# Norm factors moved into the phases before, the first token list moved ahead, and the first feed-forward's weights loaded behind the rows

## The reference

```
x = x + 0.5 * ffn(layernorm(x))
x = x + attention(layernorm(x))          # 16 heads of 16, rotary, causal
x = x + 0.5 * ffn(layernorm(x))          # the same weights as in the first

layernorm(x) = (x - mean) / sqrt(var + 1e-5)          # per token
ffn(x):   probs = softmax(x @ gate_w.T)               # 8 experts
          the two best experts of each token, their weights scaled to sum 1
          out = sum over both of weight * (silu(x @ w_gate[e]) * (x @ w_up[e])) @ w_down[e]
```

## Time and profile before

| what | value |
|---|---|
| median of 3 runs | 1222.4 us (1221.09 to 1222.83) |
| the profiled execution, its own time | 1221.54 us |
| its span (first to last instruction) | 1219.8 us |
| mean granted clock of PE | 0.906 of full speed |
| busy in the span: PE, DVE, ACT, POOL | 82%, 69%, 52%, 48% |
| SP's stores of rows (L350) | 64 of 128 KB |
| indirect DMAs: gathers, scatters | 142, 142 (both feed-forwards) |

### The profile page before, as it was taken

The page is one execution under the profiler, slowest core; times in us unless marked ns, Lnnn a source line. Parts: engine busy times, 40 slices in busy tenths (PEclk is TensorE's granted clock), DMA queues, the critical chain, the costliest instruction groups (busy, mean ns, idle before and its releaser), DMA issues. The chain is left out here.

```text
span 1219.8 us, 24054 instructions
## 1 busy us (share of the span) xinstructions
PE 1005.3 (82%) x6998; PEld 644.4 (53%) x6998; DVE 846.4 (69%) x2632; ACT 629.8 (52%) x1318; POOL 586.2 (48%) x756
## 2 busy tenths in 40 slices
PE   1639998973888389999999999999988569998850
PEld 1428987873767223333333333333348349988750
DVE  5595443434999498989998989898529784444437
ACT  1604544443777206666666666666775505544430
POOL 0937777764999402222222222222239227777740
PEclk9857999996999659999999999999989859999975
DMA  6803333324565521111111111110023413333349
GB/s 216 272 0 105 104 104 102 103 100 149 155 180 165 155 66 44 60 59 57 58 60 58 56 59 56 56 55 2 2 59 85 139 35 104 104 103 104 105 149 329
DMA packets 84524, 121.19 MB, mean 99 GB/s; under 512 B 10920, under 2 KB 63920, under 8 KB 81200
## 3 DMA queue, kind: packets, MB, share of 16 engines
q1 hardware_dynamic: 63424, 75.08, 19.7%
q0 software_dynamic: 13632, 37.24, 9.5%
q10 hardware_dynamic: 7344, 7.34, 1.8%
HBM read 75.51 MB, written 43.78 MB: 98 GB/s over the span
## 5 line engine op out<-in xcount | busy, mean ns | idle before, releaser
L1353 ACT ACTIVATE a_probs<-a_ps_s 128x1024 f32<-128x1024 f32 (+3 forms) x384 | 294.3, 813 | 172.8 <-PE a_ps_s L1385 171.6
L1268 POOL TENSOR_SCALAR_AFFINE_SELECT a_probs<-a_probs 128x256 f32<-128x256 f32 x256 | 102.8, 408 | 369.1 <-ACT a_probs L1353 366.4
L1286 DVE CUSTOM_DVE_ANT_0 a_unused<-a_ps_m,const_sb 128x128 bf16<-128x128 f32 (+3 forms) x512 | 234.1, 485 | 26.7 <-PE a_ps_m L1370 16.8
L1370 PE MATMUL a_ps_m<-st_k,st_q 96*128 96x512 bf16 (+3 forms) x768 | 219.7, 344 | 23.6 <-PEq L161 16.2
L377 POOL DMA_INDIRECT v_sb<-xn_dram,f_token_i x142 | 137.4, 968 | 100.2 <-DVE f_token_i L485 57.5
L1288 DVE TENSOR_REDUCE a_max_a<-a_ps_m 128x1 f32<-128x512 f32 x256 | 175.8, 687 | 14.0 <-PE a_ps_m L1370 13.8
L1385 PE MATMUL a_ps_s<-st_q,st_k 98*128 98x512 bf16 (+3 forms) x768 | 180.7, 329 | 1.5 <-ACT a_probs L1353 1.4
L531 DVE TENSOR_TENSOR f_h<-f_ps_gu,f_sg 128x176 f32<-128x176 f32 x142 | 48.5, 342 | 189.3 <-ACT f_sg L599 189.3
L1370 PEld LDWEIGHTS a_ps_m<-st_k,st_q 96*128 96x128 bf16 x768 | 67.8, 98 | 195.7 <-DVE a_max_a L1288 55.5
L1398 PE MATMUL a_ps_ctx<-a_probs,a_v_st 128*32 128x512 f32 (+3 forms) x1536 | 163.6, 498 | 1.3 <-POOL a_probs L1268 0.6
L381 POOL DMA_INDIRECT y_dram<-v_sb,f_pair_i x142 | 139.9, 985 | 45.3 <-issue 38.4
(11 more groups left out here) (191 smaller groups left out, 2015.6 us busy)
## 6 DMA issues: line engine op xcount, KB each, us to landing
xn_dram<-v_sb SPq DMA_DIRECT2D x64, 128.0 KB, 3.3
v_sb<-y_dram SPq DMA_DIRECT2D x32, 256.0 KB, 5.8
st_q<-qk_dram SPq DMA_DIRECT2D x16, 384.0 KB
st_k<-qk_dram SPq DMA_DIRECT2D x16, 384.0 KB
st_q<-y_dram SPq DMA_DIRECT2D x16, 256.0 KB, 3.3
st_k<-y_dram SPq DMA_DIRECT2D x16, 256.0 KB, 2.9
qk_dram<-st_rT_hi SPq DMA_DIRECT2D x16, 256.0 KB, 3.0
qk_dram<-st_rT_mid SPq DMA_DIRECT2D x16, 256.0 KB, 3.4
```

The lines of the kernel that those rows point to most:

```text
L1268: pool.affine_select(out=tri, in_=tri, compare_op=ALU.is_ge, fill=zero, base=0, pattern=[[0, 2], [1, P]], channel_multiplier=-1).then_inc( ...
L1286: dve.tensor_tensor_reduce(unused[:, bank, 0:nk], ps, cst("mask")[:, HALF - nk:HALF], 1.0, NEG, ALU.add, ALU.max, at).then_inc(taken, 1)
L1353: act.activation(probs[:, s % 4, :, 0:nq], ps_s[s % 2][:, :, 0:nq], ACT.Exp, scale=float(HD) ** -0.5).then_inc(exp_done, 1)
L1370: pe.matmul(ps_m[bank][:, 0:nk], q_st[b][0:MAX_ROW, h, P * i:P * i + P], k_st[b][0:MAX_ROW, h, k0:k0 + nk], start=True, stop=True).then_in ...
```

## The change

Three things are changed.

1. The norm factors are no longer computed at the start of a feed-forward. A class NormFactors does the same two POOL instructions for eight tiles, each pair behind a wait for DVE's moments of those tiles. In setup all four pairs stand in POOL's program, which had none. In the output projection three pairs stand inside POOL's weight split, before experts 3, 5 and 7, and the fourth behind it. ACT's wait for the factors is gone.
2. The first call of owners stands right behind later_hits(0); later_hits(1) and the four w_mix instructions follow it.
3. In the first feed-forward SP issues all 32 stores of rows first, and the 24 loads of weights behind them.

```diff
-def norm_factors(pool, own, minus_half, rstd, nmr, moments):
-    own.then_wait(pool.memset(minus_half[:], -0.5))
-    for i in range(NT // 8):
-        eight = slice(8 * i, 8 * i + 8)
-        own.then_wait(pool.tensor_tensor(rstd[:, eight], rstd[:, eight], minus_half[:], ALU.pow))
-        pool.tensor_tensor(nmr[:, eight], nmr[:, eight], rstd[:, eight], ALU.mult).then_inc(moments, 1)
+class NormFactors:
+    def __init__(self, pool, sem, var_ready, minus_half, rstd, nmr):
+        ...
+        self.own.then_wait(pool.memset(minus_half[:], -0.5))
+    def eight(self, i):
+        pool, of = self.pool, slice(8 * i, 8 * i + 8)
+        pool.wait_ge(self.var_ready, i + 1)
+        self.own.then_wait(pool.tensor_tensor(self.rstd[:, of], self.rstd[:, of], self.minus_half[:], ALU.pow))
+        self.own.inc(pool.tensor_tensor(self.nmr[:, of], self.nmr[:, of], self.rstd[:, of], ALU.mult))
...
-    def split(self, pool):
+    def split(self, pool, norm=None):
         own = Own(pool, self.own)
         for e in range(E):
+            if norm is not None and e in (3, 5, 7):
+                norm.eight((e - 3) // 2)
...
         # first feed-forward, SP
-            if load_here:
-                weights.load(sp, 0)
-                weights.load(sp, 1)
             for t in range(NT):
                 sp.wait_ge(xn_ready, t + 1)
                 sp.dma_start(xn_dram[t * P:(t + 1) * P, :], xn[:, t % 8, :]).then_inc(xn_stored[t % 8], 16)
-                if load_here and t % 4 == 3 and t // 4 + 2 < E:
-                    weights.load(sp, t // 4 + 2)
+            if load_here:
+                for e in range(E):
+                    weights.load(sp, e)
...
         # both feed-forwards, POOL
-            own = Own(pool, norm_own)
-            norm_factors(pool, own, minus_half, rstd, nmr, moments)
             if load_here:
                 weights.split(pool)
...
         # both feed-forwards, DVE
             later_hits(0)
+            dve.wait_ge(first_owned, 1)
+            owners(ps_first, 0, FIRST)
             later_hits(1)
             dve.wait_ge(egap_ready, 1)
             own.then_wait(dve.tensor_scalar(den[:], egap[:], 1.0, None, ALU.add))
...
-            dve.wait_ge(first_owned, 1)
-            owners(ps_first, 0, FIRST)
             later_hits(2)
...
         # both feed-forwards, ACT
             def normalise(t, u):
-                if u == 0:
-                    act.wait_ge(moments, t // 8 + 1)
...
         # output projection, POOL
-            weights.split(pool)
+            norm = NormFactors(pool, norm_own, var_ready, minus_half, rstd, nmr)
+            weights.split(pool, norm)
+            norm.eight(3)
...
         # setup, POOL (new)
+            norm = NormFactors(pool, norm_own, var_ready, minus_half, rstd, nmr)
+            for q in range(4):
+                norm.eight(q)
```

More of the change, by code:

```diff
@@ L123, in four, with eight @@
         dve.tensor_scalar(self.mean[:, 4 * i:4 * i + 4], self.mv[:, at:at + 4, 0], -1.0, None, ALU.mult).then_inc(var_ready, 1)
-    def eight(self, i):
+    def eight(self, i, var_ready):
         dve = self.dve
@@ L132, in eight @@
         dve.tensor_scalar(self.variance[:, bass.ds(8 * i, 8)], self.mv[:, :, 1], EPS, None, ALU.add)
-        dve.tensor_scalar(self.mean[:, bass.ds(8 * i, 8)], self.mv[:, :, 0], -1.0, None, ALU.mult)
-def norm_factors(pool, own, minus_half, rstd, nmr, moments):
-    own.then_wait(pool.memset(minus_half[:], -0.5))
-    for i in range(NT // 8):
-        eight = slice(8 * i, 8 * i + 8)
-        own.then_wait(pool.tensor_tensor(rstd[:, eight], rstd[:, eight], minus_half[:], ALU.pow))
-        pool.tensor_tensor(nmr[:, eight], nmr[:, eight], rstd[:, eight], ALU.mult).then_inc(moments, 1)
+        dve.tensor_scalar(self.mean[:, bass.ds(8 * i, 8)], self.mv[:, :, 0], -1.0, None, ALU.mult).then_inc(var_ready, 1)
+class NormFactors:
+    def __init__(self, pool, sem, var_ready, minus_half, rstd, nmr):
+        self.pool, self.own, self.var_ready, self.minus_half, self.rstd, self.nmr = pool, Own(pool, sem), var_ready, minus_half, rstd, nmr
+        self.own.then_wait(pool.memset(minus_half[:], -0.5))
[4 more added lines that the diff above has]
+        self.own.inc(pool.tensor_tensor(self.nmr[:, of], self.nmr[:, of], self.rstd[:, of], ALU.mult))
 class Semaphores:
@@ L224, in ffn_phase @@
         gu_hi, gu_lo, dn_hi, dn_lo = weights.gu_hi, weights.gu_lo, weights.dn_hi, weights.dn_lo
-        stats = sb("stats", [P, 8, 6])
-        mv = sb("mv", [P, 8, 2])
-        minus_half = sb("minus_half", [P, 8])
         xnT_at = carved[0]
@@ L306, in ffn_phase @@
         ps_later = ps_y[1][:, 0:2 * (SLOT_TILES - FIRST)]
-        norm_own = sem("norm_own")
-        stats_own, moments = sem("stats_own"), sem("moments")
         lgT_ready, lg_ready, count_ready = sem("lgT_ready"), sem("lg_ready"), sem("count_ready")
@@ L1458, in _, with output_phase @@
             turn_ctx(NGR - 1, 1, TOTAL, TOTAL % 3)
-def output_phase(nc, cst, x_sb, variance, mean, v_sb, wo_hi, wo_lo, weights, out):
+def output_phase(nc, cst, x_sb, rstd, nmr, v_sb, wo_hi, wo_lo, weights, out):
     ctx = ExitStack()
@@ L1478, in output_phase @@
         mv = sb("mv", [P, 8, 2])
-        stats_own = sem("stats_own")
+        minus_half = sb("minus_half", [P, 8])
+        stats_own, var_ready, norm_own = sem("stats_own"), sem("var_ready"), sem("norm_own")
         ps_cT = [pb(f"ps_cT{i}", [P, KD, P]) for i in range(4)]
@@ L1575, in add @@
                 dve.tensor_tensor(x_sb[:, t, :], ps_o[b][:], x_sb[:, t, :], ALU.add).then_inc(summed, 1)
-            moments_of = Moments(dve, stats_own, stats, mv, x_sb, variance, mean)
+            moments_of = Moments(dve, stats_own, stats, mv, x_sb, rstd, nmr)
             def step(i, u):
@@ L1588, in step @@
                     if u == 2:
-                        moments_of.eight(i - 1)
+                        moments_of.eight(i - 1, var_ready)
             for u in range(8):
@@ L1597, in _, with setup_phase @@
                 step(NT // 8, u)
-def setup_phase(nc, consts, x, gate_w, wq, wk, wv, wo, const_sb, x_sb, gate_sb, qkv_hi, qkv_lo, wo_hi, wo_lo, variance, mean):
+def setup_phase(nc, consts, x, gate_w, wq, wk, wv, wo, const_sb, x_sb, gate_sb, qkv_hi, qkv_lo, wo_hi, wo_lo, rstd, nmr):
     ctx = ExitStack()
@@ L1611, in setup_phase @@
         mv = ctx.enter_context(nc.sbuf_tensor("s_mv", [P, 8, 2], F32))
+        minus_half = ctx.enter_context(nc.sbuf_tensor("s_minus_half", [P, 8], F32))
+        var_ready, norm_own = ctx.enter_context(nc.semaphore("s_var_ready")), ctx.enter_context(nc.semaphore("s_norm_own"))
         x_in = [ctx.enter_context(nc.semaphore(f"s_x_in{q}")) for q in range(4)]
@@ L1639, in _ @@
                 sp.dma_start(raw[:, m, :, :], w.rearrange("(c p) h -> p c h", p=P)).then_inc(w_in[m], 16)
+        @block.gpsimd
+        def _(pool):
+            norm = NormFactors(pool, norm_own, var_ready, minus_half, rstd, nmr)
+            for q in range(4):
+                norm.eight(q)
         @block.scalar
@@ L1669, in _ @@
                     moments_of.tile(8 * q + u, u)
-                moments_of.eight(q)
+                moments_of.eight(q, var_ready)
             dve.wait_ge(turned, 1)
```

## The result

The changed kernel takes 1226.61 us in the median of 7 runs (1225.33 to 1229.74), the kernel before 1221.09 in 7 (1218.56 to 1222.83): a ratio of 1.006, 95% interval 1.0049 to 1.0072, so slower. Forecast were 1226.0, which is 3.6 above the 1222.4 known then, and slower; measured is 5.5 above 1221.09.

A forecast was written before the change was run, and what follows sets the result against it. The prediction took GpSimd's indirect gathers and scatters as the bound, so first-gather times decide. Terms +2.8 and +0.85 summed to +3.65 on 1221.54, 1225.2, or 1226.0 as the median; range 1219.5 to 1230.

The forecast's parts named there:

- GpSimd's gathers and scatters are the bound: Expert stage: 142 indirect DMAs on GpSimd, 181.67 us or 1.28 each, set its end; PE does not.
- first gather plus 182: Both feed-forwards: the expert stage ends 182 us after its first gather starts.
- Part B: Both feed-forwards: first token list ahead of later_hits(1) and w_mix; second feed-forward's first gather -2.45 us, at worst -1.85.
- the bound of 0.6: Second feed-forward: at worst one later one-hot instruction, 0.61 us, stands in the first gather's way.
- Part A in the output projection: Four factor pairs of 1.90 us in GpSimd's program make it end the phase; ACT normalises 3.3 us later.
- Part A in setup and the rows: First feed-forward: factors in setup let ACT normalise at about 28.4, not 30.55; loads behind stores start the split at 50.3.
- The split beside DVE: First feed-forward: contention with DVE lengthens GpSimd's split by 6.1 us, bounds 0 and 13.5, ending it at 91.8.
- the split is last, then a gather at 92.7: First feed-forward: the split's end, not the token list, releases the first gather, at 92.7 against 89.91, +2.8.
- rival 3: First feed-forward: DVE loses time, so the token list is last; first gather at 95.2, +5.3, total 1228.5; chance 0.10.
- the signs named for the forecast: First gather at 91 to 95 straight behind the split's L196; L492 at 2 us or more during the split; others.
- The sum: Whole kernel: +2.8 from the first feed-forward and +0.85 from the second make +3.65, a median of 1226.0 us.
- rival 2: First feed-forward: GpSimd loses each contending DVE instruction's whole length; first gather 100.1, total 1233.4; chance 0.07.

The follow-up runs named there:

- e2: The changed kernel with the factor pairs of the output projection moved back to the start of the second feed-forward; ratio 1.0046 to the kernel before.
- e5: The kernel before with only the first feed-forward's weight loads put behind all 32 row stores; ratio 1.0078 to the kernel before.
- e1: The changed kernel with the first feed-forward's weight loads back among the row stores; ratio 0.9996 to the kernel before.
- e6: Kernel before plus factors in setup, early first list, one pair inside the output projection's split, three pairs in the second feed-forward; 1213.25 us, ratio 0.9953.
- e4: The changed kernel with GpSimd splitting six of eight experts in the first feed-forward, ACT rounding the other two; one run, 1218.15 us.

## Why the prediction was right, point by point

- **GpSimd's gathers and scatters are the bound.** Right for the first feed-forward: from the first scatter to the last its stage takes 156.3 to 156.6 us in every kernel of the table, wherever it starts. In the second it takes 156.3 to 158.6, because in some executions the last scatters wait for results; there the rule "first gather plus 182" was carried over without a row.
- **Part B, -2.45.** Right: -2.39 in the changed kernel. Too small was the bound of 0.6 for gathers beside one-hot rows: 1.1 us in each feed-forward, in every kernel with the early list and in none without.
- **Part A in the output projection, +3.3.** Right: +3.29, and taken back whole in e2. GpSimd ended 3.7 us after DVE, not some 5, since DVE ended later as well: 39.20 behind the start of the split, before 37.51. Its four L132 took 0.83 us in the mean there, before 0.18; whether the pairs did that, or only where the split stood at that moment, is not shown.
- **Part A in setup and the rows.** ACT starts at 28.97 (forecast 28.4), the split at 50.86 (50.3): right.
- **The split beside DVE.** The contention term was 6.1 and measured 39.9 - 35.4 = 4.5. Of it L201 beside L491 has 4 x 0.83 = 3.3. L473 behind L491 cost GpSimd next to nothing (L203 0.67 instead of 0.61), since L201 got in between; I had counted the two as one block. The split ended at 90.8 (91.8).
- **The step that failed: the split is last, then a gather at 92.7.** The list was last. I counted what DVE takes from GpSimd and put at nothing, in the sum, what GpSimd takes from DVE, though the same row showed it: L435 lost 0.58 where the cast lost 0.19. DVE lost 13.2 us in the four lots and 9.1 before them, 22.3 in all; tensor_scalar instructions, which the sum left out, lost too (L475 took 1.24 instead of 0.29). That the split had "cost nothing" before was wrong by the 4.25 that its end took from DVE's chain. The late list was rival 3, with a chance of 0.10: it gave 95.2 for the gather and +5.3, measured 94.15 and +4.24. Its place was right, the later rows of lot 0 behind the end of the split. Two of the signs named for the forecast failed with it: the gather did not stand straight behind the split, and L491 took 1.8, not 2 or more.
- **The sum** was +3.65; the profiled executions show +5.1: 1.4 more at the first gather, 2.2 in the gathers behind, 0.5 between, and 2.8 less in the last feed-forward's tail, which I had left as it was. The total is closer than its terms, and that is luck: without the 2.8 in the tail, which no term foresaw, it would be +7.9, and between the kernel before and e5, whose second feed-forward is the same, the tail differs by 3.1.
- **The page's rule.** The Trainium skill, "SBUF — State Buffer", section "SBUF: two separate sides", has whichever of the two starts first hold the shared ports for the whole instruction, and the other blocked, also where VectorE's instruction has two inputs in SBUF. The trace agrees: L473 stood still until L201 let go, and L201, which began 0.82 behind L491 and had 1.00 of it still to run, lost 0.83. What failed is what rival 2 made of it. It charged GpSimd the whole length of every such instruction, which puts the end of the split at 99.2 instead of the measured 90.8; in turns, GpSimd loses only what is left of DVE's instruction when its own comes up, and DVE loses likewise.

## What to carry to other kernels

Work that is free on one engine is so only beside the work it stands next to now: here the end of the weight split cost DVE's chain 4.25 us before, and the whole of it 22.3 once it lay beside the choice, the ranks and the one-hot rows, so that the first gather came 8.4 (e1) to 9.2 us (e5) later than with the loads among the stores. When moving work between phases, list for both engines what lies beside it after the move, and add the loss on both sides, then ask which of the two ends last. And before putting work into another engine's program, read how long that engine's slack is (2.1 us here): one pair of 1.9 fitted and gained 2.1, four cost 3.3. A split that ends before the choice begins was not tried; in e6 the stretch from logits to first gather is 27.7 in the first feed-forward and 24.3 in the second, so some 3.4 us (an estimate from these two) still lie there.

## What the hardware showed that I had not expected

VectorE and GpSimd took strict turns at instruction grain: four lots of four instructions beside four experts of four, period 5.27 us, for 21 us on end, and lots without the split took 1.97 (e4).

The first indirect gathers are lengthened where they start behind the list that follows later_hits(0) (1.30, 0.96, 1.21, 0.95, 1.09, 1.50 in the changed kernel), but not where later_hits(1) and w_mix stand ahead of them as well (0.94 to 0.99 from the second on, before and in e5). Two of the six in the changed kernel:

```profile
97.03 1.21 POOL L376 DMA_INDIRECT v_sb<-xn_dram,f_token_i  x1 [0.30 <-issue]
...
101.19 1.50 POOL L376 DMA_INDIRECT v_sb<-xn_dram,f_token_i  x1 [0.30 <-issue]
```

It comes back in every kernel with the early list and in both feed-forwards, so it seems to hang on how the two sequences lie to each other; which DVE instruction does it was not found.
